# Delta scan: v_new copied by batch, half by VectorE and half by ScalarE, and head loads cut into pieces

## The reference, cut to what matters

```python
def step(S, inp):
    K, V, bt = inp
    A = jnp.tril(jnp.einsum('bhik,bhjk->bhij', K, K) * bt[:, :, None, :], -1)
    rhs = V - jnp.einsum('bhck,bhkv->bhcv', K, S)
    Vn = jax.scipy.linalg.solve_triangular(eye + A, rhs, lower=True)
    S = S + jnp.einsum('bhck,bhcv->bhkv', K * bt[..., None], Vn)
    return (S, Vn)
```

## Time and profile before

| | us |
|---|---|
| median of 3 timed runs | 1000.53 |
| lowest and highest of them | 997.77 and 1009.81 |
| profiled execution, its own time | 1010.85 |
| span of the profiled execution | 1008.9 |
| granted TensorE clock over that span, as a share of full speed | 0.868 |
| scan: first matmul to the end of the last copy | 193.4 to 285.3 |
| PE, DVE, ACT, POOL busy over the span | 851.9, 604.0, 460.4, 287.8 |

### The profile page before, as it was taken

How to read it: one execution, slowest core, us unless ns; L and a number is a source line. 1 busy time by engine, 2 the same in 40 slices (tenths; PEclk the granted TensorE clock), 3 DMA queues, 4 the chain that set the end, 5 groups by cost and what they waited for, 6 DMA issues and landing times. The chain is left out here.

```text
span 1008.9 us, 23678 instructions
## 1 busy us (share of the span) xinstructions
PE 851.9 (84%) x9023; PEld 604.3 (60%) x9023; DVE 604.0 (60%) x2052; ACT 460.4 (46%) x1082; POOL 287.8 (29%) x538
## 2 busy tenths in 40 slices
PE   6884823799859999999999889969899999998884
PEld 3553823788846666658896345534466666586462
DVE  1785587347757899936341634550279999384264
ACT  2564521000004777764232876463247777564054
POOL 0771231246732333330001200000023333420535
PEclk9996557858977999999697999879879999996788
DMA  6044453332310253011000000000000000190561
GB/s 128 1 108 96 142 170 126 87 74 68 92 38 2 61 174 64 2 56 41 1 1 24 6 0 1 1 0 1 1 1 2 3 2 2 35 293 10 206 233 48
DMA packets 54440, 60.55 MB, mean 60 GB/s; under 512 B 9049, under 2 KB 40247, under 8 KB 54072
## 3 DMA queue, kind: packets, MB, share of 16 engines
q1 hardware_dynamic: 43976, 44.31, 16.3%
q10 hardware_dynamic: 7488, 6.85, 2.5%
q0 software_dynamic: 2864, 7.89, 2.2%
HBM read 29.75 MB, written 25.99 MB: 55 GB/s over the span
## 5 line engine op out<-in xcount | busy, mean ns | idle before, releaser
L865 DVE CUSTOM_DVE_ANT_0 l_masked_scores<-psum,mask_q_rows 128x384 bf16<-128x384 f32 (+3 forms) x512 | 220.6, 487 | 35.5 <-PE psum L804 31.8
L882 ACT ACTIVATE l_probs<-psum 128x512 f32<-128x512 f32 (+1 forms) x384 | 174.8, 531 | 70.8 <-PE psum L790 68.7
L896 POOL TENSOR_SCALAR_AFFINE_SELECT l_probs<-l_probs 128x256 f32<-128x256 f32 x256 | 101.0, 406 | 333.1 <-ACT l_probs L882 332.3
L804 PE MATMUL psum<-kb_heads,q_heads 32*128 32x384 f32 (+3 forms) x512 | 95.8, 498 | 9.7 <-DVE l_neg_max_rows L856 8.7
L804 PE MATMUL psum<-l_k_heads,l_q_heads 32*128 32x128 f32 (+3 forms) x512 | 94.8, 495 | 3.6 <-DVE l_neg_max_rows L856 2.7
L790 PE MATMUL psum<-l_q_and_max,kb_heads 32*128 32x512 f32 (+3 forms) x512 | 88.5, 462 | 0.7 <-DVE l_q_and_max L871 0.7
L790 PE MATMUL psum<-l_q_and_max,l_k_heads 32*128 32x512 f32 (+3 forms) x512 | 87.9, 461 | 0.7 <-DVE l_q_and_max L871 0.7
L824 PE MATMUL psum<-l_probs,rows_32k 128*32 128x256 f32 (+1 forms) x1536 | 82.7, 348 | 1.3 <-POOL l_probs L896 1.3
L824 PEld LDWEIGHTS psum<-l_probs,rows_32k 128*32 128x32 f32 x1536 | 43.5, 109 | 54.3 <-POOL l_probs L896 24.6
L804 PEld LDWEIGHTS psum<-kb_heads,q_heads 32*128 32x128 f32 x512 | 58.7, 200 | 17.3 <-DVE l_neg_max_rows L856 8.9
L804 PEld LDWEIGHTS psum<-l_k_heads,l_q_heads 32*128 32x128 f32 x512 | 58.6, 200 | 11.8 <-DVE l_neg_max_rows L865 3.9
(11 more groups left out here) (355 smaller groups left out, 1751.8 us busy)
## 6 DMA issues: line engine op xcount, KB each, us to landing
sorted_scratch<-l1p_zeros SPq DMA_DIRECT2D x23, 257.0 KB, 5.9
gram_scratch<-rows_32k SPq DMA_DIRECT2D x4, 1024.0 KB, 4.9
rows_32k<-v_new_and_ones SPq DMA_DIRECT2D x64, 64.0 KB, 2.3
x_rows<-in_L_attn_x_dram SPq DMA_DIRECT2D x16, 128.0 KB, 7.3
heads_scratch<-rows_32k SPq DMA_DIRECT2D x2, 1024.0 KB, 5.4
heads_scratch<-q_kb_T SPq DMA_DIRECT2D x2, 1024.0 KB, 6.0
inverse_scratch<-block_inv SPq DMA_DIRECT2D x2, 1024.0 KB, 4.0
q_heads<-heads_scratch SPq DMA_DIRECT2D x2, 1024.0 KB, 6.7
```

Of the source, the lines that this page charges most:

```text
L804: mm = nc.tensor.matmul(ps[:, row_bank(G, u, i), o:o + w], QT(b, gq)[r, t * P:(t + 1) * P], KT(b, gq)[r, 0:w], start=True, stop=True)
L865: last = nc.vector.tensor_tensor_reduce(out=junk[:, n % 4, o:o + w], in0=ps[:, row_bank(G, u, i), o:o + w], in1=g.maskq[:, N - w:N], scale ...
L882: nc.scalar.activation(PT[:, G % 2, 2 * (u % 2) + i, o:o + w], ps[:, e_bank(G, u, i), 0:w], ACT.Exp, scale=SCALE).then_inc(x_ok, 1)
L896: last = nc.gpsimd.affine_select(out=d, in_=d, pattern=[[0, 2], [1, P]], compare_op=ALU.is_ge, fill=0.0, base=0, channel_multiplier=-1)
```

## The change

From step s = 4 on, DVE's one 128 x 512 operation is replaced by four operations of 32 partitions x 128 elements, one for each batch, which write that batch's own columns alone (the other columns of the buffer hold the zeros that the first four steps wrote there). Each multiplies by one value per partition, taken from `own`. DVE does batches 0 and 1 with `tensor_scalar`, ACT does batches 2 and 3 with `activation` (function Copy, the value as `scale`). ACT's pair raises a new semaphore `half_ok[f]`, for which PE waits ahead of line 622 and POOL ahead of its chunk, beside `vn_ok[f]`.

All head loads of batches 0 and 1 move to SP. Behind each of the chunks 0 to 11 SP issues one piece: one quarter of a batch's queries (256 KB) behind chunks 0 to 3 and 6 to 9, two of its four key loads (128 KB each) behind chunks 4, 5, 10 and 11. SP now waits for `ones_ok` ahead of its first store. The wait of the attention phase counts eight loads for batches 0 and 1.

```diff
+        half_ok = [sem(f"v_new_rows_act{f}") for f in range(2)]
+        DVE_B = 2
+        def own_rows(s, f, b):
+            r, e = slice(R * b, R * b + R), slice(HD * b, HD * b + HD)
+            src = ps[r, 4 * f:4 * f + 4, 0:2 * WB].rearrange("p j (q n) -> p j q n", q=2)[:, :, :, e]
+            return VA[r, s % NV, f, :, :, b, :], src, own[r, s % 2, HD * b:HD * b + 1]
...
                         pe.wait_ge(vn_ok[f], s + 1)
+                        if s >= NV:
+                            pe.wait_ge(half_ok[f], s - NV + 1)
...
                         dve.wait_ge(vc_ok, B * ((s - NV) // 2 + 1))
+                        for b in range(DVE_B):
+                            out, src, scale = own_rows(s, f, b)
+                            last = nc.vector.tensor_scalar(out, src, scale, None, ALU.mult)
+                        last.then_inc(vn_ok[f], 1)
+                        continue
...
         def _(act):
-            for i in range(2):
-                heads_stored(act, g, i)
-            act.wait_ge(ones_ok, 1)
-            load_heads(act, g, 1)
+            for s in range(NV, NB2):
+                for f in range(2):
+                    act.wait_ge(vn_ps[f], s + 1)
+                    act.wait_ge(vc_ok, B * ((s - NV) // 2 + 1))
+                    for b in range(DVE_B, B):
+                        out, src, scale = own_rows(s, f, b)
+                        last = nc.scalar.activation(out, src, ACT.Copy, scale=scale)
+                    last.then_inc(half_ok[f], 1)
...
                     pool.wait_ge(vn_ok[f], 2 * c + 2)
+                    if 2 * c + 1 >= NV:
+                        pool.wait_ge(half_ok[f], 2 * c + 2 - NV)
...
-            for i in range(2):
-                heads_stored(pool, g, i)
             pool.wait_ge(ones_ok, 1)
             for c in range(NT):
                 chunk(c)
-                if c in (6, 8):
-                    x = c - 6
-                    pool.dma_start(g.QS[:, 0, x:x + 2, :], g.heads_d[0].rearrange("p (x b n) -> p x b n", x=HG, b=B)[:, x:x + 2, 0, :]).then_inc(g.heads_ld[0], 16)
-                if 10 <= c < 14:
-                    load_keys(pool, g, 0, c - 10)
...
             sp.dma_start(g.maskq[:, :], g.maskq_d).then_inc(mask_ld, 16)
+            for i in range(2):
+                heads_stored(sp, g, i)
+            sp.wait_ge(ones_ok, 1)
             for c in range(NT):
                 for b in range(B):
...
+                b, x = c // 6, c % 6
+                if b < 2 and x < HG:
+                    load_queries(sp, g, b, x)
+                elif b < 2:
+                    for j in range(2):
+                        load_keys(sp, g, b, 2 * (x - HG) + j)
...
+def load_queries(eng, g, b, x):
+    eng.dma_start(g.QS[:, b % g.NS, x, :], g.heads_d[0].rearrange("p (x b n) -> p x b n", x=HG, b=B)[:, x, b, :]).then_inc(g.heads_ld[b], 16)
...
-                        pe.wait_ge(g.heads_ld[b], 16 * (5 if b else 6))
+                        pe.wait_ge(g.heads_ld[b], 16 * (8 if b < g.NS else 5))
```

## The result

The changed kernel took 1019.71 us (median of four runs, 1016.39 to 1023.40) against 1004.37 us (median of four, 997.77 to 1009.81) for the kernel before: ratio 1.0157, 95% interval 1.0109 to 1.0204. It is slower by 1.1 to 2.0%, and lies above the predicted range of 987 to 1009. The profiled execution took 1016.39 us, with a span of 1014.4 us.

A forecast was written before the change was run, and what follows sets the result against it. The first copy and then PE's own order were taken to bound each scan step. Gap -2.2, half clock -9.6 and copies +5.4 made -6.4 us; 994.1 with the half-clock stretch in the median, 1003.7 without, middle 999, range 987 to 1009.

The forecast's parts named there:

- The longer step: Scan steps with new copies: PE waits longer for the slower pair, +0.20 us a period, +5.4 us over 27 periods.
- The loads in pieces: Head loads in the scan: without the burst PE's gap goes, -2.2 us, and perhaps the half clock, -9.6 us.
- the copies' term: New copies in the scan: 27 periods at +0.20 us each, +5.4 us, bounds -1.1 and +8.4.
- the pieces' term: Head loads in pieces during the scan: -2.2 us for the gap and -9.6 us for the half clock.
- The third rival: Scan: longer waits thin PE's work, the clock falls to 0.50 and stays, 3.87 us a period; 1025 us, chance 0.04.
- The second rival: Scan: PE's gap comes from its place in the program and stays, the clock falls as before; 1005 us, chance 0.20.
- The first: Rival on the scan's copies: the pointer costs nothing beside other work, so copies get cheaper; 990 us, chance 0.22.
- The level: Before's median: with the half-clock stretch the change gives 994.1 us, without it 1003.7; the middle, 999, was taken.

The follow-up runs named there:

- e8: The whole change, but ScalarE raises VectorE's semaphore too, and TensorE and GpSimd wait once, for the sum; ratio to before 0.9995.
- e13: e3 with one wait for the sum instead of two; scan 82.8 us in one profiled execution.
- e7: The whole change, but every copy multiplies by the constant 1.0 instead of a per-partition value (different result); 1022.8 us in one run.
- e1: The change with its new copies taken back: head loads in pieces on SP, old 128 x 512 copies; ratio to before 0.9985.
- e3: The change's new copies, with all sixteen loads issued only behind the scan's last store; scan 89.3 us in one execution.
- e12: The new copies with one wait as in e8, but the old loads in a burst at the start; ratio to before 1.0291.
- e2: The change with its loads taken back to ScalarE and GpSimd, keeping the new copies; ratio to before 1.0323.
- e4: The old copies, with all sixteen loads issued only behind the scan's last store; scan 79.1 us in one execution.
- e15: e1 again, unchanged, timed in five rounds; ratio to before 0.9935.
- e9: The kernel before with four idle products instead of eight; ratio to before 1.0213.
- e5: The whole change with twelve idle products instead of eight; ratio to before 1.0050.
- e10: e1 plus a second TensorE wait, from the fifth step on, on a semaphore long raised; ratio to before 0.9987.
- e14: e4 plus a second TensorE wait on a semaphore long raised; scan 84.7 us in one execution.

## Why the prediction was wrong

**The longer step was right in size, in part by luck.** Predicted 0.35 us for each operation on VectorE and 0.37 on ScalarE, 1.49 and 1.54 for four, no overlap; measured 0.341 and 0.359, 1.43 and 1.49. TensorE was to resume at 1.55 to 1.60; it did at 1.60, because its lag behind the last copy was 0.11 us and not the 0.05 that I had taken. I took +0.20 a period and it was +0.22, 5.9 us for 5.4. But with one wait the period is 2.64 (e8, e13): the copies cost +0.13, and the other +0.09 is the second wait, which the forecast had left out. One term too high and one at nothing made up the sum. The reason for the copies' part, the pointer, is shown by e7. VectorE's four operations, each on other partitions than the one before it, took 1.43 us, 4 x 0.341 and 0.06 more: nothing overlapped. The rule of the Trainium skill ("VectorE: DVE Perf Modes", the section "Two Vector instructions with no wait between them") that the prediction weighed there agrees with that.

**The step that failed** is in "The loads in pieces": "So the gap should go: -2.2 us; and if the clock falls because of it, the other 9.6 go too." That holds for the pieces with the old copies (e1: scan 79.8, all 11.4 us won), but I added it to the copies' term as though the two were independent. They are not. The new copies bring gaps of their own through TensorE's second wait (e3 against e13, one execution each: 1.9 us of gaps and none), which need no load beside them; I had priced that wait at no more than 0.05 us a step, as a bound only, and its effect on the clock at nothing. Behind two of the gaps the clock fell, for 31 us and for the last 21 of the scan. In the place of -11.8 + 5.4 = -6.4 us, the scan got +13.1 (103.0 for 89.86), and with the second wait taken out the kernel is back at 0.9995 of before (e8). Why the clock falls behind one gap and not another isn't shown: one of 0.69 us in e3 left it at full, and one of 0.69 us in the second trace of the change is followed by half clock within 1.4 us. Nor is it shown why it then comes back in 24 to 31 us in some traces (before, the change) and not in 73 to 110 in others (e7, e12, e2).

The reading that the pieces' term leaned on was looser than it looked: the twenty steps around POOL's loads kept 2.52 us only in the mean. One of them, at s = 17, was 2.74, and 2.78 in the second trace of before.

**The third rival** had the place of the loss, the clock, and the price: 3.87 us a period at half clock for 3.94 measured. Its mechanism, "longer waits thin PE's work", is not borne out: e3, with the same longer waits, kept the full clock through the whole scan, and in the change the clock fell behind gaps. It was also all or nothing: I asked for 23 of 27 periods at half clock and gave it 0.04, with a single row (PE busy 73% in 0 to 50 us, clock 1.00) against it. Twelve periods and two partial ones came, 14.5 us and more. That row was of another kind of work and said nothing of this loop. The row that did bear on it was at hand: one gap of 2.2 us was followed by half clock for 26 us, in which TensorE was busy for 25.3 of 25.5 us. What a new gap could cost was to be read there.

**The second rival**, that the gap stays, was wrong about the burst (e1, e4: the gap goes with it). It was half right about the cause: other gaps do come by their place in the program, at the same three lines in both traces of the change. **The first** was wrong as it stood: the pointer's cost is real; without it the period does fall below before's.

**The level.** I left open whether the median of before holds the half-clock stretch. Both traces of before do; e15's 6.5 us, less than the 10 to 12 us between the profiled scans, fits executions with and without it, but that is inferred. Against two plain groups speaks that the more than sixty timed executions of before on record lie spread from 997 to 1012 us (one at 1014) without a gap of 1 us between neighbours.

## What to carry to other kernels

Splitting an operation over two engines gives the consumer a second wait: let both raise one semaphore and wait for the sum; here that was worth 1.6%. It is sound only where neither producer can get a turn ahead of the other, as here, where both wait each time for TensorE. Before making a step's copies narrower, count what doesn't shrink: the fixed part, the pointer (0.06 to 0.09 us for each) and the lost overlap between groups of partitions; four operations of a quarter's width cost more than two of the full one. And where TensorE's share of a latency-bound loop is filled up with idle products, an edit to the step, the waits or the products can cost the clock, which took 15 to 30 us of a scan of 80 here. Four products fewer cost 2.1% (e9) and four more won 1% of the change's time (e5), so try such an edit with the filling varied.

## What the runs showed that I had not expected

- Four idle products fewer (0.3 us of 2.2 us of TensorE work a step) and the clock stood at half for 105 of 108 us (e9); twelve instead of eight kept it at full in a step of 2.86 us with gaps, but for 3.4 us at its start (e5).
- After the burst's gap the kernel before won its clock back in 27 us, twice; with the new copies it did not in the 103 to 110 us left of the scan (e12, e2). Behind the smaller gaps of the change itself it took 31 and 24 us. In e7, with a shorter period than before and TensorE as busy, 73 us were not enough.
- TensorE's instruction stream can break off for 0.4 to 0.7 us inside a row of eight matmuls without any head load about (e3), and does not with one wait fewer (e13). A second wait that is already met adds nothing to the step (e10, e14).
